# Head with both table differences on GpSimd and rearranged banks, joined with token blocks of 2, 2, 4, 4, 4 tiles

## What is computed

```python
# 1: K = 2 Re(sum_n Ct exp(dtA l)), 256 channels, 64 modes, 1024 taps
K  = 2.0 * real(einsum('hn,hnl->hl', Ct, exp(dtA[:, :, None] * l)))
y  = irfft(rfft(x, 2048) * rfft(K, 2048))[:, :1024] + x * D
x  = layernorm(x + layernorm(x + y) * ln_w + ln_b)
# 2: 16 heads of 16, keys and values from ctx (2, 77, 256)
x  = layernorm(x + softmax(q @ k.T / 4) @ v @ Wo.T + bo)
# 3: feed-forward of 1024, and 1024 experts picked by two sets of 64 keys, 4 heads, top 8
mlp     = silu(x @ Wg + bg) * (x @ Wu + bu) @ Wd + bd
experts = einsum(silu(x @ down[idx]) * softmax(top scores), up[idx])
x  = layernorm(x + mlp + experts)
```

## Time and profile before

| | |
|---|---|
| median of 3 runs | 707.53 us (706.36 to 708.19) |
| profiled execution, first to last instruction | 700.8 us |
| instructions | 9712 |

### The profile page before, as it was taken

How to read it: one execution, slowest core, us unless ns; L and a number is a source line. 1 busy time by engine, 2 the same in 40 slices (tenths; PEclk the granted TensorE clock), 3 DMA queues, 4 the chain that set the end, 5 groups by cost and what they waited for, 6 DMA issues and landing times.

```text
span 700.8 us, 9712 instructions
## 1 busy us (share of the span) xinstructions
PE 590.3 (84%) x3132; PEld 383.4 (55%) x3132; DVE 506.6 (72%) x1046; ACT 404.9 (58%) x593; POOL 279.9 (40%) x333
## 2 busy tenths in 40 slices
PE   5743587785296778999999999999999999899996
PEld 2512366563264554445678565478575479453485
DVE  7999985523047885898866879767778797578783
ACT  4971655222042435797763878675579765577760
POOL 0002871635041345543343634235635234644361
PEclk9876989898596567999999999999999999999999
DMA  8945030456325000000000000000000000000000
GB/s 239 363 204 91 1 98 2 119 162 144 89 83 217 1 1 1 0 1 0 1 1 0 17 8 7 1 1 1 9 8 8 8 1 1 8 16 7 0 8 23
DMA packets 20111, 34.27 MB, mean 49 GB/s; under 512 B 7388, under 2 KB 14045, under 8 KB 18333
## 3 DMA queue, kind: packets, MB, share of 16 engines
q1 hardware_dynamic: 15677, 29.46, 13.7%
q10 hardware_dynamic: 4384, 4.20, 2.0%
HBM read 21.94 MB, written 10.65 MB: 47 GB/s over the span
## 4 chain that ended last, share of the span: by engine, by line
PE 60%; DVE 22%; ACT 7%; issue 6%; POOL 3%; DMA 1%; SPq 0%; ACTq 0%; DVEq 0%; POOLq 0%
PE banks L773 20%; PE banks L863 8%; PE banks L868 7%; PE banks L818 4%; PE banks L840 3%; PE banks L795 3%; PE banks L830 3%; PE banks L804 2%; PE banks L715 2%; DVE stats L1377 2%; ACT arena L882 2%; PE banks L651 2%; DVE arena L1468 2%; PE banks L855 2%; ACT arena L1067 1%
## 5 line engine op out<-in xcount | busy, mean ns | idle before, releaser
L1169 POOL TENSOR_TENSOR arena<-arena 128x1024 f32<-128x1024 f32 x64 | 125.8, 1965 | 156.6 <-ACT arena L1067 155.6
L773 PE MATMUL banks<-arena 128*128 128x512 f32 x384 | 174.6, 596 | 5.4 <-issue 3.7
L773 PEld LDWEIGHTS banks<-arena 128*128 128x128 f32 x384 | 69.9, 190 | 83.2 <-issue 76.5
L1067 ACT ACTIVATE arena<-arena 128x1024 f32<-128x1024 f32 x64 | 73.5, 1149 | 7.5 <-DVE arena L1466 3.2
L1069 ACT ACTIVATE arena<-arena 128x1024 f32<-128x1024 f32 x64 | 73.5, 1149 | 2.1
L1468 DVE SCALAR_TENSOR_TENSOR arena<-arena 128x1024 f32<-128x1024 f32 x48 | 63.8, 1329 | 1.7
L863 PE MATMUL banks<-arena 128*128 128x256 f32 x256 | 58.4, 381 | 2.4 <-DVE tok L1504 1.2
L957 ACT COPY arena<-banks 128x512 f32<-128x512 f32 (+1 forms) x64 | 34.1, 532 | 44.8 <-PE banks L765 29.3
L868 PE MATMUL banks<-arena 128*128 128x256 f32 x256 | 57.9, 379 | 0.0
L1142 POOL TENSOR_SCALAR arena<-mv 128x1 f32<-128x1 f32 (+1 forms) x40 | 14.1, 353 | 105.2 <-DVE mv L1378 103.8
L971 ACT ACTIVATE tok<-tok,arena,rstd 128x256 f32<-128x256 f32 x48 | 27.9, 598 | 45.5 <-POOL arena L1147 44.6
(11 more groups left out here) (179 smaller groups left out, 1077.4 us busy)
## 6 DMA issues: line engine op xcount, KB each, us to landing
scr_x<-arena SPq DMA_DIRECT2D x16, 256.0 KB, 3.2
arena<-scr_x SPq DMA_DIRECT2D x2, 2048.0 KB, 13.8
arena<-scr_z SPq DMA_DIRECT2D x32, 128.0 KB
scr_z<-arena ACTq DMA_DIRECT2D x14, 256.0 KB, 7.1
tok<-in_x SPq DMA_DIRECT2D x8, 256.0 KB, 5.7
out<-tok SPq DMA_DIRECT2D x16, 128.0 KB, 1.7
arena<-in_imat SPq DMA_DIRECT2D x1, 1152.0 KB, 5.6
arena<-in_fmat SPq DMA_DIRECT2D x1, 1088.0 KB, 7.0
```

The costliest lines, as they stand in the source:

```text
L773: ins = mm(bk[:, :], w[:, k, P * m:P * m + P], src[:, k, :], start=(k == 0), stop=(k == KC - 1))
L1067: fn(ebuf[m % 2], sxb[m % 2], ACT.Prelu, bias=negt[:, n % 2, h:h + 1], alpha=FAR).then_inc(s_ranked, 1)
L1169: tt(sxb[m % 2], sim[:, n % 2, h, 0:XR].unsqueeze(2).broadcast_to((P, XR, NKEYS)), sim[:, n % 2, FH + h, :].unsqueeze(1).broadcast_to((P, ...
```

## The change

Setup of the head:
- The parameters come in two DMAs; VectorE starts `exact_exp` behind the first.
- The growth products of `phases` move to GpSimd (`decay_steps`). Of `mode_weights`, VectorE keeps two reciprocals and four small instructions (`inverses`); the other 22 run on GpSimd (`mode_numerators`, `mode_weights`).
- `sines(0)` stands among ScalarE's copies of the x stage, behind the seventh; keys and values are copied raw out of banks 4 and 5, then `sines(1)` and the copies of `wsim` follow.
- `powers(1)` moves from before the tables to before table 4, `context` from before the tables to behind the last spectra.

Tables and spectra:
- Both differences of a table run on GpSimd.
- `taps` of one group and `x_second` share two pairs of banks in turns (0, 1 and 4, 5); both halves of a group are copied together, 4 copies a group instead of 8, and `x_second` has one copy instead of two.
- Orders change: `x_second` behind taps 2, 3, 4, 5 and 6; `k_first` of the first half behind four of them, before taps 4; spectra of the first half as soon as the last table's products are done; `values` and `x_bias` behind all spectra.
- The inverses alternate between two pairs of banks throughout, `zring` has 8 places, `scr_z` keeps the order of rows in which `zB` is read, and SP reads it in 5 batches a half instead of 16 planes.
- SP's round trip of the values stands behind these reads.

Body:
- Token blocks have 2, 2, 4, 4 and 4 tiles (`BLOCKS`) instead of 4, 4, 4, 4. Wide matmuls, evacuations and gates of a block of two have 256 columns.
- Attention of tile t stands at `ATTEND_AT[t]`: one tile a slot, but tiles 4 to 7 at half a slot each. Feed-forward of tile t stands at slot t + 2. So the plan has 18 slots instead of 20.
- Layer norms of tile pairs 4 to 7 stand later, at 2.3, 3.2, 4.1 and 4.9.

The core of the diff:

```diff
-ZRING = 4
+ZRING = 8
+SHIFT_X = 6
+BLOCKS = ((0, 2), (2, 2), (4, 4), (8, 4), (12, 4))
+ATTEND_AT = (0, 1, 2, 3, 4, 4.5, 5, 5.5, 6, 7, 8, 9, 10, 11, 12, 13)
+FEED_AT = (2, 3, 4, 5, 6, 7, 8, 9, 10, 11, 12, 13, 14, 15, 16, 17)
-         "ln": (-1.672, -1.4042, 0.3146, 1.2224, 1.9378, 2.3695, 3.0308, 3.1386),
+         "ln": (-1.672, -1.4042, 0.3146, 1.2224, 2.3, 3.2, 4.1, 4.9),
-         "taps": (0.982,), "x_second": (-0.756, 0.69), "skip": (0.382,), "k_first": (5.96, 0.01, 9.6, 0.059),
-         "simw": (-1.866,), "x_bias": (2.891, 0.086), "values": (2.518,), "diagonal": (-1.627,),
+         "taps": (0.982,), "x_second": (3.4, 4.05, 4.1, 4.15, 4.2, 5.4, 6.4, 7.4, 7.45), "skip": (0.99,),
+         "k_first": (4.5, 0.01, 8.52, 0.1),
+         "x_bias": (11.0, 0.1), "values": (11.5,),
...
+def z_batches():
+    return [(0, 3), (3, 5), (5, 7), (7, 8), (8, 9)]
...
         def z_bank(m):
-            return 2 * (m % 2) if m >= FREQ else 0
+            return 2 * (1 - m % 2)
+        def unit_bank(key):
+            return 4 * (1 - UNIT_AT[key] % 2)
...
-            for n in range(2 * FREQ):
-                hf, k = divmod(n, FREQ)
-                sp.wait_ge(s_zw[n % ZRING], 16 * z_writes(n + 1, n % ZRING))
-                for r in tiles_of(k):
-                    sp.dma_start(zB[NS * r:NS * r + NS, hf].rearrange("s h q n -> s h (q n)"),
-                                 scr_z[hf, r].rearrange("(h s q) n -> s h (q n)", h=2, s=NS)).then_inc(s_zr[hf], 16)
+            for hf in range(2):
+                for k0, k1 in z_batches():
+                    for n in range(FREQ * hf + k0, FREQ * hf + k1):
+                        sp.wait_ge(s_zw[n % ZRING], 16 * z_writes(n + 1, n % ZRING))
+                    r0, r1 = NS * tiles_of(k0)[0], NS * (tiles_of(k1 - 1)[-1] + 1)
+                    sp.dma_start(zB[r0:r1, hf].rearrange("r h q n -> r (h q n)"),
+                                 scr_z[hf, r0:r1].rearrange("r c n -> r (c n)")).then_inc(s_zr[hf], 16)
+            sp.wait_ge(s_kbz, 1)
+            sp.dma_start(t["scr_v"].rearrange("b h k d -> k (b h) d"), ...)
...
             for j in range(4):
-                ins = nc.scalar.copy(ktime[:, :, ch + j:ch + CH:4], src[HALF * j:HALF * j + HALF, HALF * j:HALF * j + HALF, :])
+                rows_of = slice(HALF * j, HALF * j + HALF)
+                src = banks[rows_of, b0:b0 + 2, :].rearrange("p h (k c) -> p c h k", c=P)
+                ins = nc.scalar.copy(by_half[:, :, :, ch + j:ch + CH:4], src[:, rows_of])
...
+            mode_numerators()
+            decay_steps(0)
+            mode_weights()
+            decay_steps(1)
             for kind, n in order(HEAD, "pool"):
-                elif kind == "tables":
+                if kind == "tables":
+                    v, u = power[n % 2]
                     pool.wait_ge(s_uterm, n + 1)
                     tt(u, u, u_terms[n % 2], ALU.subtract).then_inc(s_utab, 1)
+                    pool.wait_ge(s_vterm, n + 1)
+                    tt(v, v, v_terms[n % 2], ALU.subtract).then_inc(s_tab, 1)
...
             phases(0)
             phases(1)
-            mode_weights()
+            inverses()
             powers(0)
-            dve.wait_ge(s_ce, KC)
-            powers(1)
-            context()
             for kind, n in order(HEAD, "dve"):
                 if kind == "tables":
+                    if n == HALF_GROUPS:
+                        dve.wait_ge(s_ce, KC)
+                        powers(1)
                     tables(n)
                 elif kind == "spectra":
                     spectra(*divmod(n, FREQ))
+            context()
```

395 lines of the change are left out of this document (212 added, 183 removed).

## The result

The changed kernel takes 758.4 us (median; runs from 756.0 to 761.9), the kernel before, beside it, 707.9: a ratio of 1.075, 95% interval 1.067 to 1.083. It is slower; 678 with a range of 656 to 697 was forecast. Some executions of a kernel are slower as a whole: ratios and intervals leave them out, medians hold them all. The profiled execution took 756.0 us, its span is 754.2 (before: 700.8).

A forecast was written before the change was run, and what follows sets the result against it. It took the head to be bound by a chain through several engines, attention alone by no full engine, and the rest by TensorE. 700.8 - 21.2 - 34.4 + 26.1 = 671.3, plus 6.7 gives 678 us; range 656 to 697.

The forecast's parts named there:

- mixed stretch: From feed-forward's start to the first turn of the first block of four: 132 us instead of 105.9, +26.1.
- +3.8 +9.3 us: VectorE in the mixed stretch: 48 half-width steps replacing 24 cost 3.8 us, gaps between 280 instructions 9.3.
- A pair of norms 5.2: VectorE load in the mixed stretch: each pair of layer norms takes 5.2 us, four pairs 20.8.
- Mixed stretch stalls: Rival: half-length slots and block edge 2 stall the mixed stretch, 150 us there, 696 in all; chance 0.14.
- Slower: Rival: attention keeps 27.8 us a tile even in half slots, six tiles take 167 us, 713 in all; chance 0.05.
- Token blocks, first turn to feed: Body start: feed-forward can start after two tiles, 43 us after the first turn instead of 77.4, -34.4.
- Setup and contention: Head setup: VectorE's two-SBUF-input steps and GpSimd's run one after the other; first table at 48, not 57.4.
- the clean rival: Clean overlap: the lock rarely bites, tables at 40, mixed stretch at 122 us, 660 in all; chance 0.24.
- Tables to last inverse: Head, from first table at 48 through spectra to the last inverse: ends at 152 instead of 169.4.
- z transport: Head, z planes out and back between last inverse and convolutions: 10.5 us instead of 18.8, from 0.8 + 4.6 + 5.
- Values: Value round trip behind the z reads delays the first turn by 4.5 us, on 14.6 from the convolutions.
- From span to median: Last term: the median of the runs lies 6.7 us over the profiled span, making 671.3 into 678.

The follow-up runs named there:

- f2: e8 with four added groups of useless 512-column matmuls in front of the four largest waits of its mixed stretch: 721.1 us, ratio 1.027.
- e8: Changed kernel with 256-column wide steps joined in pairs and the last four layer-norm pairs back at their earlier places: 719.3 us, ratio 1.018.
- e10: e1 with TensorE allowed only two wide steps of 512 columns ahead instead of three: 738.0 us, ratio 1.043.
- e14: Changed kernel with paired wide steps, TensorE held to two units ahead where both are wide feed-forward steps of blocks of two: 737.8 us, ratio 1.055.
- f4: e8 with the first two layer norms of tiles 8 to 15 left out, a bound that doesn't compute the layer: 716.4 us, ratio 1.017.
- e9: e8 with one tile of attention in each slot instead of half slots: 729.0 us, ratio 1.033.
- e4: Changed kernel with one tile of attention in each slot instead of half slots: 757.6 us, ratio 1.074.
- e1: New head with the body of the kernel before (blocks of four, old slots and layer-norm places): 690.1 us, ratio 0.987.
- e13: e1 with the second table difference (v) moved from GpSimd back to VectorE: 689.4 us, ratio 0.984.
- e7: e1 with context between the halves of the spectra and the whole value round trip between the two halves of z reads: 690.4 us, ratio 0.978.
- e11: As e7, but only the value write stands between the z-read halves; its reads back precede the last two z reads: 689.1 us, ratio 0.984.

## Why the prediction failed, point by point

**The failed step is the mixed stretch**, "So VectorE becomes late next here, with TensorE at 94% beside it" and 132 us. I summed busy times, found 129 for the fuller engine and added 3. The sum itself was nearly right: its busy part, without the 9.3 us between instructions, is 119 for VectorE and measured 117. The stretch took 204, so it was not an engine's load that decided; the step that failed is the overlap, that two engines' work would interleave within 3 us of the fuller one. Of the 72 us over forecast, TensorE's idle time is 53 where 12 were allowed (41), and its busy time 151 where 120 were (31). The second is the lower clock behind the gaps (0.82 x 151 = 124), and only a part of it lengthens the stretch: f2 gave back 8 us in e8's first two slots, of which 2.5 to 4 were on the chain. What was missing:
- Work ahead. I priced 256-column steps only in VectorE's fixed costs (+3.8 +9.3 us) and wrote that they "cost TensorE nothing extra". They cost it half of what three banks hold. Pairing them gave 23 us; e10 and e14 showed the mechanism apart from instruction counts, at 39 to 52 us (all units of the three banks, the whole body) and 8 us (four slots).
- Order. "A pair of norms 5.2" was charged as load. Its load is nearly free (f4), its place in front of an expert step, of GpSimd's sums or of a bank's reader is not: 9 us alone, 13 with pairing.
- What is left. e8 still takes 168 us where TensorE's need was put at 120 and f2 confirms the size (52.5 us near full clock for two slots, where 2 x 80.4 / 4 and 2 x 7.3 make 54.8). Excluded for most of these 36 to 48 us: the norms (f4) and the half slots (e9); the clock has 2.5 to 4 us in the first two slots (f2), and wasn't tried in the other two. More than three units ahead were not tried either. What may remain is the length of each tile's chain through four in-order queues, similarity to outer product, which in a block of two has no neighbour to hide behind. That is argued, not shown.

**The rivals.** "Mixed stretch stalls" had the right mechanism in general words and a bound of 150. "Slower" named one tile per 27.8 us in the half slots as its place and 161 us as its turning point; the stretch passed that point, but e9 (and e4, less sharply) shows the half slots to be innocent. The first two mixed slots, at 41.9 us a tile, had no rival at all. The bound of 150 was half the way to 167, taken without a row; the row that spoke against it stood in the earlier trace rows, 77.4 us for four tiles with TensorE busy 58.9: a chain that leaves TensorE idle even with nothing beside it.

**Token blocks, first turn to feed**: 43 forecast, 44.2 measured. Right, by its own steps.

**Setup and contention**: first table product forecast at 48, measured at 45.3 (before 57.4). One after the other holds where the two met: VectorE's product of 128 columns, 0.29 us undisturbed, took 2.86 us and ended 0.2 us behind GpSimd's growth product of 2.81; GpSimd's steps of 128 columns, 0.45 us undisturbed, took up to 1.85 beside VectorE. Where they met was not as priced: the phases ended at 22.3, as if alone (22.5), and not at 27.3, because GpSimd began its first steps only at 18.1 and the growth product at 22.7; instead the six steps took 5.9 us and not 3.2. The growth product was 2.81 and not 3.45 us, 0.6 too high each, and the nineteen steps should have been added up to 10.0 and not 9.5. The Trainium skill (SBUF — State Buffer, section "SBUF: two separate sides") says an exclusive lock, held for the whole instruction, and so do these rows; the clean rival (38.1) is out.

**Tables to last inverse**: 152 forecast, 155.2 measured, from a start 2.7 us earlier, so 6 us lost on the way. The first inverse of the first half, forecast for 113.4, started at 113.4, so 2.7 of them were lost before it and 3.2 behind it; where, no run tells, and with the same head e1 and e13 end this part at 158. The gain of four steps instead of five was none (e13), as the text had suspected for the second half only.

**z transport**: 13.3 us idle instead of 10.5 (before 18.8). The last z write was issued at 155.7, and SP, which waited for it, issued the last read at 163.9: the write took 8.3 us, the longest of the 18, where I took 4.6 from before. The read took 4.5 us, where I took 5. So the term that was too small is the write; the read was right. Why that write was slow stays open; the slowest z write takes 6.4 to 9.3 us in all profiles with this order of reads.

**Values**: 20.7 us from convolutions to first turn, 19.1 forecast, 14.6 before. The delay is 6.1 us, the upper end of my "2.6 to 6", where I took 4.5; in e1, with the same head, it is 3.4, so the term moves from execution to execution by more than I missed it. What I hadn't seen is that neither of the two other places tried would hide it (e7, e11).

Head in sum: -13.6 instead of -21.2 us, as 3.2 + 2.8 + 1.6 = 7.6.

**From span to median**: the 6.7 us added at the end were 4.2 here (758.4 - 754.2); that term was 2.5 too large and brought the forecast nearer by as much, by luck.

## What to carry to other kernels

A stretch in which no engine is full is not bounded by the fuller engine plus a little: count how many microseconds of work the bound engine can have ahead (buffers times the work in one), and compare that with the longest burst that stands in front of the step that frees a buffer, on every in-order engine. Making the unit of work smaller shrinks the first and leaves the second; pair units to keep a buffer full. And a low clock beside idle time is first a symptom: fill the gaps once to see what it is worth before blaming it, with fills shorter than the gaps, and look on the chain, not at the whole stretch, for what it gave.
